# One or two gate and up pairs tile by tile at the start of a two-layer kernel

## What is computed

```python
xn = _layernorm(x)
x = x + _L0_attn_ref(xn, ...) + _L0_ffn_ref(xn, ...)      # layer 0
xn = _layernorm(x)
x = x + _L1_attn_ref(xn, ...) + _L1_ffn_ref(xn, ...)      # layer 1

# _L0_attn_ref: h = xn @ Win.T + bin; then four times: layernorm, silu, a scan over the
#   sequence, layernorm, a feed-forward of width 256; at the end layernorm and Wout
# _L0_ffn_ref, with ternary weights:
gate_out = x_flat @ gate_w.T          # 512 -> 1792
up_out = x_flat @ up_w.T              # 512 -> 1792
hidden = jax.nn.silu(gate_out) * up_out
out_flat = hidden @ down_w.T          # 1792 -> 512
```

## Time and the profile before

| what | value |
|---|---|
| median of 3 runs | 300.22 us (300.07 to 300.53) |
| time of the profiled execution | 300.16 us |
| its span, first to last instruction | 298.4 us |
| PE busy | 288.8 us, 97% |
| DVE busy | 173.6 us, 58% |
| POOL busy | 161.2 us, 54% |
| ACT busy | 120.8 us, 40% |
| mean granted TensorE clock | 1.00 of full |

### The profile page before, as it was taken

How to read it: one execution, slowest core, us unless ns; L and a number is a source line. 1 busy time by engine, 2 the same in 40 slices (tenths; PEclk the granted TensorE clock), 3 DMA queues, 4 the chain that set the end, 5 groups by cost and what they waited for, 6 DMA issues and landing times.

```text
span 298.4 us, 4397 instructions
## 1 busy us (share of the span) xinstructions
PE 288.8 (97%) x1580; PEld 191.9 (64%) x1580; DVE 173.6 (58%) x267; ACT 120.8 (40%) x201; POOL 161.2 (54%) x185
## 2 busy tenths in 40 slices
PE   8798989999999999999999999989999999999995
PEld 6695447565556666565565645646587888788784
DVE  4695984657348684655645447779869621333303
ACT  1537734626532131644436454022066720245500
POOL 3878998254975202355444469510566583067640
PEclk9999999999999999999999999999999999999999
DMA  7994891870000111010111001300020001100003
GB/s 260 285 223 151 128 189 35 126 117 9 0 0 25 48 43 66 0 48 0 37 35 29 0 37 44 98 0 2 0 71 0 3 1 70 72 1 0 2 0 141
DMA packets 11749, 17.86 MB, mean 60 GB/s; under 512 B 848, under 2 KB 6224, under 8 KB 11728
## 3 DMA queue, kind: packets, MB, share of 16 engines
q1 hardware_dynamic: 6624, 12.49, 12.7%
q0 software_dynamic: 4960, 4.98, 10.9%
q10 hardware_dynamic: 144, 0.12, 0.1%
HBM read 20.46 MB, written 2.10 MB: 76 GB/s over the span
## 4 chain that ended last, share of the span: by engine, by line
PE 85%; DVE 9%; POOL 2%; ACT 1%; DMA 1%; issue 1%; DVEq 0%; POOLq 0%
PE bank L705 15%; PE bank L598 14%; PE bank L599 14%; PE bank L566 9%; PE bank L568 8%; PE bank L567 8%; PE bank L664 5%; PE bank L636 3%; PE bank L642 2%; PE bank L627 2%; PE bank L560 1%; PE bank L654 1%; PE bank L655 1%; DVE st L906 1%; DMA X<-in_x 1%; DVE X L1079 1%
## 5 line engine op out<-in xcount | busy, mean ns | idle before, releaser
L1196 POOL TENSOR_TENSOR hidl<-hid,hidh 128x512 f16<-128x512 f32 x28 | 32.6, 1167 | 48.1 <-ACT hidh L771 47.9
L598 PE MATMUL bank<-xh,gatew 128*128 128x512 f16 (+1 forms) x136 | 43.9, 342 | 0.4 <-DVE xl L933 0.3
L598 PE MATMUL bank<-xh,upw 128*128 128x512 f16 (+1 forms) x136 | 43.9, 341 | 0.0
L599 PE MATMUL bank<-xl,gatew 128*128 128x512 f16 (+1 forms) x136 | 43.9, 341 | 0.0
L599 PE MATMUL bank<-xl,upw 128*128 128x512 f16 (+1 forms) x136 | 43.9, 341 | 0.0
L1202 POOL TENSOR_TENSOR actl<-hid,acth 128x512 fp32r<-128x512 f32 (+1 forms) x22 | 28.6, 1305 | 26.2 <-ACT acth L778 26.0
L705 PE MATMUL bank<-downw,hidh 128*128 128x512 f16 x112 | 42.5, 380 | 0.0
L705 PE MATMUL bank<-downw,hidl 128*128 128x512 f16 x112 | 42.5, 379 | 0.0
L1104 POOL TENSOR_TENSOR root<-var,powers 128x4 f32<-128x4 f32 (+1 forms) x25 | 23.5, 942 | 26.1 <-DVE var L967 18.6
L1036 DVE SCALAR_TENSOR_TENSOR hid<-bank,early,silu 128x512 f32<-128x512 f32 x28 | 21.0, 751 | 19.2 <-PE bank L599 18.8
L851 ACT ACTIVATE silu<-bank,early 128x512 f32<-128x512 f32 x28 | 19.2, 686 | 31.9 <-PE bank L599 31.9
(11 more groups left out here) (161 smaller groups left out, 610.2 us busy)
## 6 DMA issues: line engine op xcount, KB each, us to landing
X<-in_x SPq DMA_DIRECT2D x8, 256.0 KB, 5.8
out_x<-X SPq DMA_DIRECT2D x8, 256.0 KB, 2.0
downw<-in_down POOLq DMA_DIRECT2D x2, 896.0 KB, 8.8
stage<-in_v SPq DMA_DIRECT2D x6, 256.0 KB, 2.6
stage<-in_mask SPq DMA_DIRECT2D x4, 256.0 KB, 6.4
gatew<-in_gate POOLq DMA_DIRECT2D x1, 1024.0 KB, 9.0
upw<-in_up POOLq DMA_DIRECT2D x1, 1024.0 KB, 13.8
stage<-in_weight SPq DMA_DIRECT2D x4, 256.0 KB, 2.5
```

The costliest lines, as they stand in the source:

```text
L598: pe.matmul(bank_of(key)[:, c], w, xh[b][:, k, c], start=(k == 0), stop=False)
L599: mm = pe.matmul(bank_of(key)[:, c], w, xl[b][:, k, c], start=False, stop=(k == KT - 1))
L1196: pool.tensor_tensor(hidl[:, n % FT, :], hid[:, n % UNITS, :], hidh[:, n % FT, :], ALU.subtract).then_inc(hid_lo, 1)
```

## The change

Only pair 0 is worked out tile by tile. The four steps `("first", t, 1)` leave the prologue, and with `FIRST = 1` dense slots 2 and 3 (gate 1 and up 1) are normal slots of 512 columns on PE, behind `win`. Banks 2 and 3, which pair 1 had, go to the transposes of tiles 0 and 1, whose banks 4 and 5 go to pair 1. No other step moves in the list.

```diff
-FIRST = 2
+FIRST = 1
...
             (("xt", 1), ("codes", 1), ("first", 0, 0), ("norm", 3), ("load", 1), ("grow", 1)),
-            (("xt", 2), ("rows", 0), ("first", 0, 1), ("xcopy", 0), ("first", 1, 0), ("grow", 2), ("grow", 3)),
-            (("xt", 3), ("centre", 0), ("first", 1, 1), ("xcopy", 1), ("first", 2, 0), ("first", 2, 1), ("xcopy", 2),
-             ("first", 3, 0), ("first", 3, 1), ("xcopy", 3)))
+            (("xt", 2), ("rows", 0), ("xcopy", 0), ("first", 1, 0), ("grow", 2), ("grow", 3)),
+            (("xt", 3), ("centre", 0), ("xcopy", 1), ("first", 2, 0), ("xcopy", 2),
+             ("first", 3, 0), ("xcopy", 3)))
```

## The result

| what | before | after |
|---|---|---|
| median | 300.22 us (300.05 to 300.53, 5 runs) | 301.68 us (301.64 to 302.02, 5 runs) |
| ratio | | 1.0054, 95% interval 1.0043 to 1.0065 |
| time of the profiled execution | 300.16 us | 301.68 us |
| its span | 298.4 us | 299.9 us |
| PE busy | 288.8 us | 288.4 us |

The change costs 1.46 us by the medians and 1.52 by the profiled executions. The forecast was 1.7 (301.9, range 300.9 to 303.3). Of some kernels further on, some executions spent part of their time at a lower granted clock: the ratios leave out those with a mean clock of 0.983 or less, and "undisturbed" means a mean clock of 0.998 or more.

A forecast was written before the change was run, and what follows sets the result against it. PE's program in its order was taken as the bound: -3.54 removed, +2.86 prologue idle, +3.45 added give +2.77; -0.91 and +0.50 give +2.36; -1.08 and +0.42 at `z` give +1.70. Predicted 301.9 us, range 300.9 to 303.3.

The forecast's parts named there:

- Prologue: PE's four removed steps (3.54 us) leave 2.86 us idle; last tile step stays at 17.71, `win` comes 0.68 us earlier.
- First stall taken back: PE's 0.91 us wait ahead of block 1's first transpose goes, cutting its lateness from 2.77 to 1.86 us.
- The new wait: Ahead of block 1's second transpose, PE waits about 0.5 us for ACT's work behind silu 2; lateness 2.36 us.
- The stretch of DVE: DVE's unbroken work from 28.33 to `z` starts at 30.46, 2.13 us late; gains beside POOL decide the rest.
- the table cost the same: In DVE's stretch, rot meets POOL's hidl 1 instead of its DMA issues, and is assumed to cost the same.
- the cast half a microsecond less: In DVE's stretch, the W1 cast begins at about 34.8 and waits half a microsecond less beside POOL's hidl 2.
- The lateness behind `z`: PE's lateness after `z` lies between 1.28 and 2.13 us, taken as 1.7.
- Behind `z`: From 40.30 on, no PE stall gives anything back; the one at 195.74 moves along, so lateness stays.
- PE itself is ready for z at 41.58, so 1.28 at the least: PE can start `z` at 41.58 once its 1.08 us wait is used up, so lateness is at least 1.28 us.
- Rival 1: Nothing is handed back: an added ACT or DVE collision keeps PE 2.77 us late; 302.9, up to 303.3; chance 0.09.
- rival 3: Not slower: the branch sets the first 40 us and its stalls close; 300.2 (chance 0.09) or faster, 299.3 (0.06).
- Rival 2: The granted clock falls to 1.2 GHz in the thinned prologue, slowing `win`: 305.6 us (303.5 to 309); chance 0.07.

The follow-up runs named there:

- run 1: Kernel after, with the four removed pair 1 steps (64 matmuls) put back in the prologue as filler whose result nobody reads: 302.35 us, ratio 1.0076.
- half kernel: Half of the change against the kernel before: gate 1 stays tile by tile, only up 1 is a wide slot behind `win`; 301.56 us, ratio 1.0049.
- runs 3 and 4: Both W1 casts moved from ahead of `z` to behind the first scan: in the kernel after 301.6 to 301.8 us (undisturbed), in the kernel before 300.13.
- Run 8: Kernel after, with `win` and its ln moved from 1.6 to 3.6, behind the two wide slots of pair 1: 301.59 us, ratio 1.0045.
- the run at 0.978: Profiled execution, at mean granted clock 0.978, of the kernel after with both W1 casts and the w2 centring moved out of DVE's stretch: 306.17 us.
- run 5: Kernel before, with both W1 casts and the w2 centring moved behind the last xl of block 1, out of DVE's stretch: 298.85 us, ratio 0.9954.

## Why the prediction was right

- **Prologue.** No release in it came from the removed matmuls: right. Last tile step forecast for 17.71, `win` 18.80, gate 2 25.97; with 0.15 added it was 17.71, 18.84, 26.00. The filler run confirms the reading from the other side.
- **First stall taken back, a part returned.** Forecast lateness 1.86, then 2.36; measured 1.89, then 2.35. The new wait was forecast at 0.5 and is 0.41 by the shown ends, 0.57 with the 0.16.
- **The stretch of DVE.** Forecast start 30.46, measured 30.45. I let the table cost the same (2.06 us; it took 2.17) and the cast half a microsecond less (0.61 less). The first of these two terms was an assumption that came out, with luck: in the half kernel two of the three table instructions are hindered, and `t1` waits 0.9 us for it. That the cast would meet less of hidl 2 was worked out, and it did. The lateness behind `z` was forecast at 1.70 and is 1.65 in the profile; the 0.15 of the earlier start makes 1.5 of it. That the medians differ by 1.46 and not 1.65 I do not read further: single executions of one kernel differ by 0.3.
- **Behind `z`.** Here the working had a gap that cost nothing. It said that nothing there could give something back. There was a second wait on the same stretch, `win` of block 1 at 44.8, then only about 0.1 us, and runs 3 and 4 show that it takes over what `z` gives up. My bound "PE itself is ready for z at 41.58, so 1.28 at the least" was therefore not a bound on the time: with the wait at `z` taken away the kernel after stays at 301.7.
- **Rival 1** is out, **rival 3** is out: behind the first stall (0.91 us, which is gone) only the wait at `z` gave something back, 0.67 us of its 1.08, and the stall ahead of 37.03 stayed. Run 8 shows that an early `win` buys next to nothing. **Rival 2** was given 0.07. It is not what the five runs behind the result show, but it is real: 10 of 34 executions of this kind, and 1 of 10 of the kernel after. The clock fell in the run at 0.978 in a stretch with two transposes and one tile step. The Trainium skill, "TensorE: Matmul & The Clock Gate", section "Part 4: PE-mode transpose", says that transposes do not count as PE activity as other matmuls do. The trace does not contradict it and does not show it: 23 of the 24 other executions of this kind had the same transposes and a mean clock of 0.998 or more, and no run takes the transposes alone away.

## What to carry to other kernels

Small pieces of work that fill an engine's idle time at the start are worth what they fill, not what they cost: 3.54 us of matmuls cost 0.67 there (run 1), and the same products cost 3.45 of PE's time once they stand behind `win`. Before a stall further on is counted as giving something back, follow the releasing engine to the end of its unbroken stretch and list every exit of it that somebody waits for; a job moved from one exit to the next gains nothing (runs 3, 4), three moved out of the stretch gained 1.4 us (run 5). And where a change thins TensorE's work early on, take several executions and look at each one's granted clock before believing a median.

## What was not expected of the hardware

- One and the same DVE instruction of 128x256 on SBUF operands takes 0.41 to 0.43 us or 0.93 to 1.43, the latter only with a GpSimd instruction beside it, and which of three in a row is hindered differs between kernels whose stretches start at other times. DVE's same 18 instructions took 15.98 us in the half kernel and 14.79 in the kernel after.
- The lower clock, once granted at 14.9 us, held for more than 13 us, though PE was busy throughout every window of it from 18 us on, and so cost 4.9 us.
